# Rounding by writing int16: the step's instruction goes, the floor of the largest value becomes a 257th number of each row, GpSimd multiplies twice

## The reference, cut to what matters

```
def _absmax_scale(x, axes):
    amax = jnp.max(jnp.abs(x), axis=axes, keepdims=True)
    return jnp.maximum(amax, 1e-12) / 127.0
lhs_scale = _absmax_scale(lhs, (2,))          # lhs = layernorm(h), one scale per token
rhs_scale = _absmax_scale(rhs, (0,))
q_lhs = clip(round(lhs / lhs_scale), -127, 127).astype(int8)
q_rhs = clip(round(rhs / rhs_scale), -127, 127).astype(int8)
acc = dot_general(q_lhs, q_rhs, int32)
h = h + acc.astype(float32) * lhs_scale * rhs_scale
```

## Time and profile before

| | |
|---|---|
| median of three runs | 103.8 us |
| span of the profiled execution, first to last instruction | 102.7 us |
| around the span (median less span) | 1.1 us |
| busy: TensorE / VectorE / ScalarE / GpSimd | 92.3 / 82.5 / 76.1 / 70.1 us |
| first `scale` stage starts | 44.1 us |
| last VectorE instruction | 100.08 us |

### The profile page before, as it was taken

One profiled execution on the slowest core, in us unless ns is written; L12 is line 12 of the kernel. 1 busy time (PEld: TensorE's weight loads), 2 busy tenths in 40 slices (PEclk: granted clock), 3 DMA queues, 4 the chain that ended last, 5 costly groups with the idle time before them and its releaser, 6 DMA issues.

```text
span 102.7 us, 2135 instructions
## 1 busy us (share of the span) xinstructions
PE 92.3 (90%) x686; PEld 83.8 (82%) x686; DVE 82.5 (80%) x224; ACT 76.1 (74%) x150; POOL 70.1 (68%) x133
## 2 busy tenths in 40 slices
PE   5999994999997999978989989999999788998870
PEld 5988894999696999968979969998897667987650
DVE  3377694489979988996999999899978988998731
ACT  1328646989996999938889987967698999927510
POOL 2000056979458709998997859998998959899940
PEclk9999999999999999999999999999999999999998
DMA  3999992679899999199993896788000230002513
GB/s 71 290 286 377 253 307 99 175 255 324 145 204 206 263 284 203 24 179 317 249 332 136 134 198 179 126 209 169 13 31 0 105 133 3 6 0 97 191 50 132
DMA packets 8137, 17.35 MB, mean 169 GB/s; under 512 B 855, under 2 KB 4799, under 8 KB 8127
## 3 DMA queue, kind: packets, MB, share of 16 engines
q0 software_dynamic: 2880, 10.49, 43.5%
q1 hardware_dynamic: 4815, 6.47, 19.9%
q10 hardware_dynamic: 432, 0.27, 0.9%
HBM read 14.81 MB, written 2.41 MB: 168 GB/s over the span
## 4 chain that ended last, share of the span: by engine, by line
ACT 23%; POOL 19%; PE 16%; DVE 13%; DMA 11%; issue 10%; SPq 4%; POOLq 0%; ACTq 0%
DMA x_sb<-x_dram 11%; POOL rstd L400 7%; ACT xn L619 4%; ACT x_low L523 4%; POOL rstd L399 4%; POOL x_high L425 4%; SPq L350 3%; DVE stats L694 3%; PE h_ps L1003 3%; ACT convT L573 2%; POOL shift L448 2%; ACT xc L629 2%; DVE amax L809 2%; ACT tmp L531 2%; ACT glob L603 2%
## 5 line engine op out<-in xcount | busy, mean ns | idle before, releaser
L908 PE MATMUL h_ps<-w_high,x_high 128*128 128x256 f32 x112 | 33.8, 302 | 0.1
L912 PE MATMUL h_ps<-w_high,x_low 128*128 128x256 f32 x112 | 31.3, 280 | 0.0
L910 PE MATMUL h_ps<-w_low,x_high 128*128 128x256 f32 x112 | 31.3, 279 | 0.0
L908 PEld LDWEIGHTS h_ps<-w_high,x_high 128*128 128x128 f32 x112 | 21.1, 188 | 1.0 <-issue 0.8
L910 PEld LDWEIGHTS h_ps<-w_low,x_high 128*128 128x128 f32 x112 | 21.1, 189 | 0.2
L912 PEld LDWEIGHTS h_ps<-w_high,x_low 128*128 128x128 f32 x112 | 21.1, 188 | 0.0
L399 POOL TENSOR_SCALAR rstd<-mv 128x2 f32<-128x2 f32 (+2 forms) x21 | 8.6, 410 | 17.4 <-DVE mv L697 16.7
L400 POOL TENSOR_TENSOR rstd<-rstd,exponent 128x2 f32<-128x2 f32 (+2 forms) x21 | 16.8, 798 | 1.8
L694 DVE BATCH_NORM_STATS2 stats<-h_ps 128x6 f32<-128x256 f32 (+1 forms) x36 | 13.8, 420 | 2.9 <-PE h_ps L912 1.6
L619 ACT ACTIVATE xn<-h_ps,shift,rstd 128x256 f32<-128x256 f32 x16 | 8.1, 559 | 6.3 <-POOL shift L448 6.3
L781 DVE SCALAR_TENSOR_TENSOR convT<-xnT,par_sb,convT 128x255 f32<-128x255 f32 (+1 forms) x24 | 12.2, 550 | 0.5 <-ACT convT L573 0.3
(11 more groups left out here) (109 smaller groups left out, 205.0 us busy)
## 6 DMA issues: line engine op xcount, KB each, us to landing
x_high<-x_dram POOLq DMA_DIRECT2D x10, 512.0 KB, 6.4
x_low<-x_dram POOLq DMA_DIRECT2D x10, 512.0 KB, 6.1
x_sb<-x_dram SPq DMA_DIRECT2D x4, 512.0 KB, 9.0
out_dram<-fin SPq DMA_DIRECT2D x8, 256.0 KB
x_sb<-x_dram SPq DMA_DIRECT2D x3, 256.0 KB, 4.3
par_sb<-par_dram SPq DMA_DIRECT2D x1, 325.0 KB, 8.4
txt_sb<-txt_dram SPq DMA_DIRECT2D x1, 308.0 KB
out_dram<-fin SPq DMA_DIRECT2D x4, 77.0 KB
```

The source lines that it names most:

```text
L908: nc.tensor.matmul(h_of(g)[:, t, :], x_high[:, g % RING, kc, at], w_high[:, kc, :], start=(kc == 0 and t == 0), stop=False, skip_group_che ...
L910: nc.tensor.matmul(h_of(g)[:, t, :], x_high[:, g % RING, kc, at], w_low[:, kc, :], start=False, stop=False, skip_group_check=True)
L912: last = nc.tensor.matmul(h_of(g)[:, t, :], x_low[:, g % RING, kc, at], w_high[:, kc, :], start=False, stop=(kc == KC - 1), skip_group_che ...
```

## The change

`LOW_ZERO` and the tile `nstep` go. `xc` gets 257 numbers a row; the last one is written once, at the start, with the floor 1e-12 * sqrt(1e-5), and the reduction of `scale` reads all 257, so the floor is inside the maximum. `scale` is then two instructions, and `qmul` is the reciprocal of `amax` itself, positive. The factor 127 comes in as the second multiplication of `round`, whose output `v` is now an int16 tile, so that the rounding is done by writing it; the transposes read `v` densely, and `ints` is a plain copy. `lscale` is amax times the factor, and the missing -1/127 is folded into `rs_row`. Since `v` and `lscale` have both changed sign, the product is the same.

```
-        nstep = sb("nstep", [P, ITEMS, 2])
-        xc = sb("xc", [P, 4, 2, D])
-        v = sb("v", [P, 2, 2, D])
+        xc = sb("xc", [P, 4, 2, D + 1])
+        v = sb("v", [P, 2, 2, D], I16)
-        v_low = v[:, :, :, :].bitcast(BF16).rearrange("p n t (d h) -> p n t d h", h=2)
+        v16 = v[:, :, :, :].bitcast(BF16)
...
-                    nc.gpsimd.tensor_tensor(lscale[0:rows, j, 0:nt], nstep[0:rows, j, 0:nt], rstd2[0:rows, j, 0:nt],
+                    nc.gpsimd.tensor_tensor(lscale[0:rows, j, 0:nt], amax[0:rows, j, 0:nt], rstd2[0:rows, j, 0:nt],
...
-                        last = nc.gpsimd.tensor_scalar(v[0:rows, j % 2, t, :], xc[0:rows, j % 4, t, :],
-                                                       qmul[0:rows, j, t:t + 1], ROUND + LOW_ZERO,
-                                                       ALU.mult, ALU.add)
+                        last = nc.gpsimd.tensor_scalar(v[0:rows, j % 2, t, :], xc[0:rows, j % 4, t, 0:D],
+                                                       qmul[0:rows, j, t:t + 1], INT8_MAX, ALU.mult, ALU.mult)
...
-                                         ACT.Copy, bias=-LOW_ZERO).then_inc(qT_ready, 1)
+                                         ACT.Copy).then_inc(qT_ready, 1)
...
+            nc.vector.memset(xc[:, :, :, D:D + 1], SCALE_FLOOR * LN_EPS ** 0.5).then_inc(floor_ready, 1)
...
-                nc.vector.tensor_scalar(rs_row[:, :], acc_ps[:, 0:D], -1.0, None,
+                nc.vector.tensor_scalar(rs_row[:, :], acc_ps[:, 0:D], -1.0 / INT8_MAX, None,
...
-                    a, am, qm = (z[0:rows, j, 0:nt] for z in (amax, nstep, qmul))
+                    a, qm = (z[0:rows, j, 0:nt] for z in (amax, qmul))
+                    if j == 0:
+                        dve.wait_ge(floor_ready, 1)
                     dve.wait_ge(xc_ready, j + 1)
                     then_wait(nc.vector.tensor_reduce(a, xc[0:rows, j % 4, 0:nt, :], AX_X, ALU.max,
                                                       apply_absolute_value=True))
-                    then_wait(nc.vector.tensor_scalar(am, a, SCALE_FLOOR * LN_EPS ** 0.5, -1.0 / INT8_MAX,
-                                                      ALU.max, ALU.mult))
-                    nc.vector.reciprocal(qm, am).then_inc(qmul_ready, 1)
+                    nc.vector.reciprocal(qm, a).then_inc(qmul_ready, 1)
```

More of the change, by code:

```diff
@@ L19 @@
 ROUND = 12582912.0
-LOW_ZERO = 16384.0
 STEP = 16
@@ L277, in early_fusion_kernel @@
         txt_cleared = sem("txt_cleared")
+        floor_ready = sem("floor_ready")
         exponent_ready = sem("exponent_ready")
@@ L628, in _ @@
                     for t in range(nt):
-                        last = nc.scalar.activation(xc[0:rows, j % 4, t, :], h_item(j)[0:rows, t, :],
+                        last = nc.scalar.activation(xc[0:rows, j % 4, t, 0:D], h_item(j)[0:rows, t, :],
                                                     ACT.Identity, scale=-1.0, bias=mv2[0:rows, j, t, 0:1])
@@ L1026, in q_turn @@
                         last = nc.tensor.transpose(q16_v[:, c, t * P:t * P + rows],
-                                                   v_low[0:rows, j % 2, t, c * P:(c + 1) * P, 0],
+                                                   v16[0:rows, j % 2, t, c * P:(c + 1) * P],
                                                    ident16[0:rows, 0:rows])
```

## The result

The changed kernel takes 103.18 us (median of 20 runs, 102.01 to 105.16) against 104.03 of the kernel before in the same series; the ratio is 0.991, 95% interval 0.988 to 0.994, that is 0.96 us less, 0.7 to 1.2. In a second series on one chip the ratio of the same two kernels was 1.001 (0.997 to 1.005). The intervals don't overlap; weighted by the inverse squares of their widths the two give 0.994, some 0.7 us. The ratios compare only the runs within 1.5% of the fastest of each kernel, and part of the gap between the two series comes from that cut: the means over all runs give 0.993 and 0.997. Faster, then, but by how much the times alone don't settle. The profiles settle more.

What follows compares the result with a forecast made beforehand. TensorE, busy 92.3 of 102.7 us, was taken as the bound, so only its few waits and the tail pay. 0.34 + 0.12 + 0.2 + 0.17 = 0.83 us off gives span 101.9, plus 1.1 around it 103.0; range 102.4 to 104.3.

Steps and rivals of the forecast that it cites:

- The mechanism: The small tensor_scalar on VectorE waits out whatever GpSimd runs, 0.17 against 0.71 us; the reciprocal doesn't wait.
- the dearer int16 write: Rival, chance 0.15: GpSimd writes int16 v more slowly, up to 0.25 us each; 105.5 us, at half of it 104.2.
- the wait that passes on: Rival, chance 0.10: the reciprocal now meets GpSimd's instruction and waits; gain 0.36 us, time 103.4.
- (a): Item 3: v starts sooner without the tensor_scalar, and TensorE's 0.39 us gap before the transposes shrinks; gain 0.34 us.
- (b): Group 5's chain to the adding DMA for group 7's second half: DMA some 0.45 us sooner, net gain 0.12.
- its rival: Chance 0.17: the adding DMA doesn't come sooner, so TensorE loses item 3's gain there; 0.1 to 0.37 in all, 103.6.
- The prediction's own sign of being wrong: Wrong if L467 grows by over 0.08, or group 7's product gap grows by what (a) gave.
- (c): Group 7: statistics start with the token product's end, so `xn` and the turn come sooner; gain 0.2 us.
- (d): Tail: GpSimd's list alone sets item 10's v, which no longer waits for the reciprocal; gain 0.17 us.
- The sum: 0.34 + 0.12 + 0.2 + 0.17 = 0.83 us gained, giving 103.0 us.

Runs made afterwards that it cites:

- c2: Changed kernel with a second reciprocal, into a spare tile, where the removed 128x2 tensor_scalar stood; ratio to the kernel before 0.992 (0.988 to 0.996).
- c3: Changed kernel with the old 128x2 tensor_scalar put back in its place, into a spare tile; ratio to the kernel before 1.000 (0.996 to 1.004).
- c1: Kernel before with the int16 write of v alone, its tensor_scalar step and 256 numbers kept; ratio to the kernel before 0.996 (0.992 to 1.000).
- c4: Changed kernel with v written in fp32 as before, factor 127 left out; ratio to the kernel before 0.993 (0.989 to 0.997).
- c5: Changed kernel with 256 numbers a row, without the floor and its memset; ratio to the kernel before 0.996 (0.992 to 1.001).
- c9: Changed kernel with the old 128x2 tensor_scalar back for item 3 alone, into a spare tile; ratio to the kernel before 0.996 (0.991 to 1.001).
- c0: The changed kernel again, without an edit, as reference in the second series; ratio to the kernel before 1.001 (0.997 to 1.005).
- c8: Changed kernel with the adding DMA of group 7's second half placed ahead of item 1's last addition; ratio to the kernel before 0.997 (0.992 to 1.001).
- c7: Changed kernel with item 7's last addition on VectorE instead of GpSimd, ahead of item 9's `out`; ratio to the kernel before 0.992 (0.988 to 0.996).
- c11: c10 without the two matmuls on ones ahead of item 11's transposes; ratio to the kernel before 0.996 (0.993 to 1.000).
- c10: Changed kernel with item 7's last addition at the end of GpSimd's list, its store between items 10 and 11; ratio to before 0.992 (0.987 to 0.997).
- c12: c10 with item 7's last addition cut in two, one half in GpSimd's idle time ahead of item 10's v; ratio to before 0.993 (0.989 to 0.997).

## Why the prediction was right

103.0 was forecast, 103.2 came, 0.8 less against 0.96 (0.7 to 1.2) in the ratio; the second series, with 1.001, shows no gain. The steps one by one, by the intervals:

- **The mechanism.** Shown by c2 against c3: the step is costly because it waits for GpSimd; c1, c4 and c5 show no price or gain of the rest of the change. The rivals of the dearer int16 write and of the wait that passes on are refuted: 478 ns, and a reciprocal of 0.159 to 0.167 us in all twelve items. One reading of the rows was too neat: of the four long steps, the one of 46.47 ends at 46.95 with no GpSimd instruction; the two v beside it end at 46.76 and 47.21.
- **(a)** 0.34 was forecast, item 3's transposes came 0.24 sooner (14.08 to 13.84). L479 ends where the working had it (12.74 behind group 3's turn, before 12.75), but v starts 0.10 behind that end (59.60 to 59.70), not with it: this is the term that was too large. The gap left is 0.13, not under 0.1.
- **(b)** 0.12 net was forecast. At group 5's turn another 0.17 had been won (17.87 to 17.46): the weight load's wait of 0.21 for `xn` (the row of c1 above; before has it too), which the working had left out. c9 shows that (a) and this, all but 0.07, come from item 3's step alone. The adding DMA was issued 0.66 sooner, 65.26 - 46.86 = 18.40 against 65.55 - 46.49 = 19.06, more than the 0.45 assumed. It landed 0.31 sooner in this execution (26.12 against 26.43) and 1.22 sooner in c0 (25.21). But what was late next was not foreseen: the first half's DMA, at the start of group 7's product. In the two executions it landed 0.24 and 0.11 sooner and TensorE came 0.4 sooner; the gap there is 0.28 to 0.59 in the nine profiles without the step that have the old order of the DMAs (0.76 in c8). Net, from group 5's to group 6's turn, 11.59 became 11.72 in one execution of the changed kernel and 11.33 in the other: minus 0.13 to plus 0.26, against the step's 0 to 0.24 and its rival. The prediction's own sign of being wrong, a gap in group 7's product grown by what (a) gave, is there in the profile after: 0.29 at the beginning and 0.29 in the middle, against 0.30 before. In c0 the 0.30 became 0.41.
- **(c)** 0.2 was forecast. Between the turns of groups 6 and 7 before takes 4.22, after 4.06. The statistics now wait for TensorE (0.66 idle at 76.22), as the step said. But c1 and c3 take 4.07 and 4.06 with the step in place, their product ending later: the gain is there only where VectorE is behind the product. Right in size for the profile of before, and conditional.
- **(d)** 0.17 was forecast, the tail is 0.13 shorter (19.91 to 19.78), and the kernels c1 to c8 fall on the same two sides but for c7. That GpSimd's list alone sets this tail was too simple: v of item 11 doesn't set item 11's output, item 10's `out` does, which has to free the accumulator bank first (99.00 to 99.10 in the profile after, and c11). c10 brings v of item 10 forward by 0.35 and the last VectorE instruction by 0.31, but then the last stores (c10, c12) are what ends last. And the new collision shown under c9 takes back some 0.1 of the gain in this term.
- **The sum.** 0.83 was forecast; up to the last VectorE instruction 0.58 and 0.95 were measured in two executions, and 0.91, 0.86 and 0.19 in c2, c4 and c5, whose steady intervals are the same. That the total comes so near is in part luck: the 0.17 at group 5's turn, which the working left out, makes up for what (a), (c) and (d) fell short (0.10, 0.04 and 0.04), and the landing of the second half's DMA decides over more than any of them. VectorE's busy time fell by 2.8 us, not by 3.4: L781, untouched, went from 12.2 to 12.7.

What stays open is what holds back the second half's DMA. From issue to landing it takes 6.5 to 8.0 us in the fourteen profiles, the first half's 5.4 to 5.9. In all six profiles in which it takes 7.3 us or more, 16 KB of instructions were fetched by the DMA engines meanwhile, but so they were in two in which it takes 6.8 or less (c2, c11); no run tests it.

## What to carry to other kernels

Look at a group's longest instance, not its mean: a 128x2 tensor_scalar of 0.17 us that sometimes takes 0.7 waits for something, and if it stands in a chain that others wait for, dropping it or putting an operation that doesn't wait in its place can pay more than its own duration: here the one instance at item 3 was worth 0.35 to 0.4. By c7 and c9 the exclusion works both ways, so a piece of work moved from GpSimd to VectorE should not be one with two SBUF inputs beside a GpSimd instruction on the path. Placing a DMA earlier in a list helps only where its input is ready: the one of c8 started 0.04 us sooner. Where executions scatter by more than the effect, count from a point behind the scatter to a point behind the edit.

## What the runs showed of the hardware

- A tensor_scalar of 128x2 in SBUF on VectorE, 0.17 us where it is undisturbed, waits until the running GpSimd instruction has ended (0.70 us beside L480 in c3); one of 0.48 beside two short ones, at the start of the second layer, ends with neither. A reciprocal (0.17) and a tensor_reduce of 128x514 (0.69 beside L479 in the profile after, 0.68 on the mean) at such places don't wait. The Trainium skill, "SBUF — State Buffer", the section on ports, has the lock for two-port modes and for two SBUF inputs; that a reciprocal takes none is c2's finding.
- From the other side: beside a VectorE instruction with two SBUF inputs, v took 0.98 instead of 0.48 (c7), and a GpSimd tensor_scalar of 77x1 0.58 instead of 0.23 (c0 against c9). In c12 the same pair started together and VectorE's took 0.54 instead of 0.49 and GpSimd's 0.23.
- A wait that the profile labels "issue" can be the landing of a DMA: in fourteen profiles the gaps in group 7's product end 0.10 to 0.11 us behind it.
- GpSimd writes 256 numbers of int16, rounded, as fast as fp32: 478 ns at the median for both, with a multiply and an add or two multiplies.
- The start of group 3's turn lies between 44.85 and 47.25 us in the twelve profiles with that column here, whatever the edit. Most of the spread of the times is there already when the second layer begins, and hardly any of it is in the steady intervals.
